# A decoder block on one core: x1 filled by its own transfer, out rows on ScalarE, a_ylo on VectorE, and a new order of steps

## What is computed

```python
x = x + attn(layernorm(x), w_attn, w_proj)              # 16 heads, causal linear attention, phi = elu + 1
x = x + xattn(layernorm(x), ctx, ctx, W_diff, ...)      # tanh-probabilities of q and ctx, softmax(-sid / 16) @ ctx,
                                                        # W_diff, layernorm, MLP 256-1024-256 with gelu, layernorm
x = x + ffn(layernorm(x), w_router, W_qkv, ...)         # out = h, but the 128 of 256 rows with the highest router
                                                        # score are replaced by h + attention + gated MLP of them
```

## Time and profile before

| | |
|---|---|
| median of 3 runs | 922.85 us (919.57, 922.85, 923.87) |
| profiled execution | 919.85 us; its span, first to last instruction, 918.0 us |
| PE busy | 817.0 us, 89% of the span |
| DVE busy | 725.8 us, 79% |
| ACT busy | 577.3 us, 63% |
| POOL busy | 301.5 us, 33% |
| DMA | 39.82 MB, 43 GB/s over the span (292 GB/s in the first fortieth) |
| granted TensorE clock | 0.98 of full speed on the mean |

### The profile page before, as it was taken

How to read it: one execution, slowest core, us unless ns; L and a number is a source line. 1 busy time by engine, 2 the same in 40 slices (tenths; PEclk the granted TensorE clock), 3 DMA queues, 4 the chain that set the end, 5 groups by cost and what they waited for, 6 DMA issues and landing times.

```text
span 918.0 us, 21136 instructions
## 1 busy us (share of the span) xinstructions
PE 817.0 (89%) x7222; PEld 705.6 (77%) x7222; DVE 725.8 (79%) x1609; ACT 577.3 (63%) x1550; POOL 301.5 (33%) x443
## 2 busy tenths in 40 slices
...
GB/s 292 84 47 1 59 24 47 41 35 48 6 81 6 57 29 46 40 29 51 6 80 6 57 29 46 40 29 51 6 80 6 57 29 46 30 2 46 6 53 7
DMA packets 26871, 39.82 MB, mean 43 GB/s; under 512 B 2256, under 2 KB 18768, under 8 KB 26832
## 3 DMA queue, kind: packets, MB, share of 16 engines
...
## 4 chain that ended last, share of the span: by engine, by line
PE 35%; DVE 22%; issue 17%; POOL 11%; ACT 10%; DMA 3%; POOLq 1%; SPq 0%; DVEq 0%; ACTq 0%
PE bank L1117 10%; DVE a_s L867 4%; PE bank L1239 3%; ACT w_raw_or_stage_c L712 3%; PE bank L1221 2%; DMA x_in<-in_x 2%; PE bank L1301 2%; ACT L712 2%; PE bank L1309 2%; PE bank L1401 2%; PE bank L1279 2%; PE bank L1385 2%; PE bank L1396 2%; POOL f_rs L436 1%; DVE prob L908 1%
## 5 line engine op out<-in xcount | busy, mean ns | idle before, releaser
L675 ACT ACTIVATE prob<-bank,b_folded 128x256 f32<-128x256 f32 x128 | 53.8, 471 | 111.4 <-PE bank L1117 111.2
L867 DVE TENSOR_TENSOR a_s<-bank,const 128x512 f32<-128x512 f32 x112 | 72.6, 685 | 40.0 <-PE bank L1239 21.7
L712 ACT ACTIVATE w_raw_or_stage_c<-bank,c_nmax 128x128 f32<-128x128 f32 x256 | 91.7, 406 | 3.2 <-DVE c_nmax L1037 3.0
L451 POOL TENSOR_TENSOR a_tr_lo<-a_norm,a_tr_hi 128x512 fp32r<-128x512 f32 x16 | 20.6, 1285 | 141.2 <-ACT a_tr_hi L562 141.2
L712 ACT ACTIVATION_READ_ACCUMULATOR w_raw_or_stage_c<-bank,c_nmax 128x1 f32 x256 | 62.7, 245 | 0.0
L784 DVE TENSOR_TENSOR b_s_lo<-prob,b_s_hi 128x512 fp32r<-128x512 f32 x64 | 44.9, 701 | 17.3 <-ACT b_s_hi L562 17.3
L427 POOL TENSOR_TENSOR q_bias<-b_f,vectors_by_row 128x512 f32<-128x512 f32 x16 | 20.6, 1285 | 114.4 <-DVE b_f L933 114.4
L1037 DVE TENSOR_REDUCE c_nmax<-bank 128x4 f32<-128x512 f32 x64 | 41.1, 685 | 21.0 <-PE bank L1401 21.0
L857 DVE RECIPROCAL a_e<-a_e 128x512 f32<-128x512 f32 x16 | 53.5, 3346 | 0.0
...
L1117 PE MATMUL bank<-b_s_hi,w_mlp_hi 128*128 128x256 f32 x256 | 45.1, 298 | 2.7 <-ACT prob L675 1.4
L1117 PEld LDWEIGHTS bank<-b_s_hi,w_mlp_hi 128*128 128x128 f32 x256 | 34.4, 188 | 13.0 <-issue 10.4
...
## 6 DMA issues: line engine op xcount, KB each, us to landing
...
```

Source lines behind the costliest of these rows:

```text
L675: act_in(prob[:, 2 * (j % 2) + n, :], b0[:, n * T:(n + 1) * T], ACT.Gelu, bias=b1p[:, f:f + 1]).then_inc(b_gelu.sem, 1)
L712: act_in(c_e[g % 2][:, j * R:(j + 1) * R], C_SCORES[g][:, j * R:(j + 1) * R], ACT.Exp, bias=c_nmax[:, n:n + 1], accum_out=c_den[:, head:he ...
L867: tt(heads(A_MASKED[t][n][:, :]), heads(A_SCORES[n][:, :]), tri.unsqueeze(1).broadcast_to([P, 4, P]), ALU.mult).then_inc(a_scput.sem, 1)
```

## The change

Four things are changed at once:

1. `x1` is no longer copied by GpSimd. SP loads it from memory a second time (`keep_x`), once at the start, and then behind `b_kept` and `b_normed` of the sequence before. `next_x` no longer waits for the copy.
2. `c_ob` moves to ScalarE. x2 + (x2 - mean) * r is computed as x2 * (1 + r) - mean * r in two activations with a factor and an offset per row; GpSimd makes factor and offset in a new step `c_obs` of three small instructions.
3. `a_ylo` moves to VectorE.
4. `ORDER` is new, and with it the places in `WARM_AT` (72 matmuls before, 74 after). `WEIGHTS_AT` is the same table.

```diff
+            sp.dma_start(x1[:, :, :], x_rows[0]).then_inc(a_kept.sem, 16)      # behind the loads of raw, ahead of ctx
...
             def next_x(b):
                 sp.wait_ge(*a_normed(b))
                 sp.sem_inc(passed.sem, 1)
-                sp.wait_ge(*a_kept(b))
+                sp.dma_start(xin[:, :, :], x_rows[b + 1]).then_inc(x_in.sem, 16)
+
+            def keep_x(b):
+                sp.wait_ge(*b_kept(b - 1))
                 sp.sem_inc(passed.sem, 1)
-                sp.dma_start(xin[:, :, :], x_rows[b + 1]).then_inc(x_in.sem, 16)
+                sp.wait_ge(*b_normed(b - 1))
+                sp.sem_inc(passed.sem, 1)
+                sp.dma_start(x1[:, :, :], x_rows[b]).then_inc(a_kept.sem, 16)
...
                 store(i - 2)
+                keep_x(i)
                 next_ctx_t(i - 1)
...
-            def a_kept_(b):                                                     # gpsimd
...
-                nc.gpsimd.tensor_copy(x1[:, :, :], xin[:, :, :]).then_inc(a_kept.sem, 1)
...
-            def a_ylo_(b):                                                      # gpsimd
-                pool.wait_ge(*a_yhi(b))
-                low(flat(a_tr[1][:, :, :]), flat(a_norm[:, :, :]), flat(a_tr[0][:, :, :]), a_ylo)
...
-            def c_ob_(b):                                                       # gpsimd
-                pool.wait_ge(*c_normed(b))
...
-                nc.gpsimd.tensor_tensor(ob[:, :, :], x2, c_norm, ALU.add).then_inc(c_ob.sem, 1)
+            def c_obs_(b):
+                pool.wait_ge(*c_rstd(b))
+                if not first(b):
+                    pool.wait_ge(*c_ob(b - 1))
+                pool.sem_inc(passed.sem, 1)
+                nc.gpsimd.tensor_scalar(c_gain[:, :], c_rs[:, :], 1.0, None, ALU.add).then_inc(c_obs.sem, 1)
+                nc.gpsimd.tensor_tensor(c_offset[:, :], c_mv[:, :, 0], c_rs[:, :], ALU.mult).then_inc(c_obs.sem, 1)
+                pool.wait_ge(*c_obs(b, 2))
+                pool.sem_inc(passed.sem, 1)
+                nc.gpsimd.tensor_scalar(c_offset[:, :], c_offset[:, :], -1.0, None, ALU.mult).then_inc(c_obs.sem, 1)
...
+            def c_ob_(b):                                                       # scalar
+                act_e.wait_ge(*c_obs(b))
+                if not first(b):
+                    act_e.wait_ge(*out_done(b - 1))
+                for t in range(TT):
+                    act_in(ob[:, t, :], x2[:, t, :], ACT.Identity, bias=c_offset[:, t:t + 1], scale=c_gain[:, t:t + 1]) \
+                        .then_inc(c_ob.sem, 1)
...
+            def a_ylo_(b):                                                      # vector
+                dve.wait_ge(*a_yhi(b))
+                low(flat(a_tr[1][:, :, :]), flat(a_norm[:, :, :]), flat(a_tr[0][:, :, :]), a_ylo)
...
                     dve.wait_ge(*c_rms1(b - 1))                                 # c_mean
+                    dve.wait_ge(*c_obs(b - 1))
...
-                    dve.wait_ge(*c_ob(b - 1))                                   # c_normed
```

One line of `ORDER` each, the part of a round with `c_idx` and `b_dtp`:

```diff
-a_val c_idx a_qout b_diff b_frstd+ b_dtp c_put++ c_gu_1+ b_rtp a_rstd a_ylo+ c_rank b_log c_gu_2+ c_gtp_0+
+c_idx c_gu_1+ b_vput b_dtp c_normed b_diff c_h2sq+ c_rscore b_rtp c_h2hi+ b_vq c_rank c_gu_2+ c_hx+ c_sel
```

More of the change, by code:

```diff
@@ L44 @@
 ORDER = """
-c_w2 a_kput+ c_ff_0++ c_ff_1++ c_gtlo_1++ c_rstd+ c_ht+ a_score_0+ b_fput+ b_fmean+ b_htp+ a_sput+ c_hsc+
-b_sexp+ c_gthi_0++ b_fnormed+ c_gthi_1++ a_mask+ a_mean a_dput+ c_w7 a_scput_0+ b_hlo+ a_scput_1+ c_qk+
-c_hput+ c_w1 b_up_0+ a_scput_2+ a_scput_3+ a_score_1+ c_w3 c_y++ c_rms1+ c_v+ a_scput_4+ b_hhi+ a_att_0+ c_w4
-c_qkput+ b_gelu_0+ a_scput_5+ a_scput_6+ b_up_1+ a_scput_7+ a_att_1+ b_ghi_0+ b_gelu_1+ b_glo_0+ a_dinv+
-c_vput+ a_y+ b_glo_1+ b_ghi_1+ b_down_0+ b_up_2+ b_gelu_2+ c_score+ b_up_3+ c_w8 a_proj+ a_yhi+ b_ghi_2+ c_w9
@@ L50 @@
-c_h2rms++ c_max_0+ c_max_1+ b_down_1+ b_down_2+ b_gelu_3+ b_qb+ c_etp_0+ c_max_2+ c_exp_0+ c_hx++ b_down_3+
-b_glo_2+ a_done+ c_max_3+ b_ghi_3+ c_exp_1+ c_etp_1+ c_ob+ b_v b_mean c_exp_2+ a_tp b_glo_3+ a_normed b_normed
-b_kept+ c_etp_2+ c_etput_0+ c_w0 c_exp_3+ c_w5 b_o+ c_etp_3+ c_dtp+ c_att+ b_omean+ b_onormed+ c_dinv+ b_done+
-c_etput_1+ c_xo+ c_dbc+ c_mean c_keep+ c_pick+ c_o+ c_etput_2+ a_tlo c_etput_3+ c_normed c_h2put+ c_dput+ a_q
-a_thi b_tanhk b_tanhq c_h2tp+ a_kept+ c_h2sq+ a_k c_rscore b_pnorm c_sbc c_gu_0+ c_h2lo+ b_vput b_fb2+ c_h2hi+
@@ L55 @@
-a_val c_idx a_qout b_diff b_frstd+ b_dtp c_put++ c_gu_1+ b_rtp a_rstd a_ylo+ c_rank b_log c_gu_2+ c_gtp_0+
-c_sel a_ktp b_vq b_sid c_gtp_1+ a_state b_rstd b_fd c_idxput b_orstd+ c_tanh_0+ a_kout b_ratio c_gate_0+
-a_phi_q a_phi_k b_dput c_gate_1+ b_rput c_w6 a_csum a_kq c_gtlo_0+ c_tanh_1+ a_den a_vput
+c_qk+ c_gtlo_1++ b_up_0+ c_w2 a_kput+ a_score_1+ c_hsc+ a_sput+ b_fnormed+ a_scput_0+ a_mask+ a_scput_1+
+b_hlo+ a_dput+ c_v+ c_hput+ b_frstd+ a_scput_2+ a_scput_3+ c_w7 b_hhi+ a_mean a_att_0+ c_w1 a_scput_4+ c_y++
```

37 lines of the change are left out of this document (22 added, 15 removed).

## The result

| | before | after |
|---|---|---|
| median, first comparison | 922.73 us (919.57 to 923.87, 4 runs) | 890.44 us (888.23 to 896.51, 4 runs) |
| ratio | | 0.9665 (95%: 0.962 to 0.9709) |
| the changed kernel again (e1) | 920.00 us | 889.39 us, ratio 0.9660 (0.9628 to 0.9692) |
| a round in the loop | 51.65 | 49.62 |

The forecast was 908.2 us with a range of 895 to 922: the direction is right, the size is wrong. 13 us were forecast, 31 to 32 came.

The account below looks back on a forecast made before the run. TensorE was taken to bound a round (48.13 of 51.68 us busy). Thirteen rounds at -1.2 (-15.6), fill -0.9 and drain +3.2 gave -13.3, from 921.5 to 908.2 us; range 895 to 922.

Parts of the forecast that it names:

- The two waits of 0.55 (b_dtp) and 0.79 (a_ktp): TensorE's waits for the copied-out index and for kT; both were to go in each round, -0.55 and -0.79.
- b_diff: VectorE step, to take 0.7 beside a short GpSimd instruction instead of 1.45 beside a long one.
- c_max_1 and c_dinv: VectorE steps: c_max_1 done at 451.7, about when ScalarE comes to the exponentials; c_dinv delays b_done 0.8; both priced 0.
- The wait for b_s_lo: New TensorE wait of 0.4 at the last pass of b_down_3, from VectorE's longer queue behind c_max_0.
- The lock rival: b_diff waits up to 0.7 for a short GpSimd instruction; scores late at c_sbc, +0.6 a round: 916.6 us; chance 0.04.
- c_att: TensorE's attention product: its 0.52 wait takes up the 0.4 delay of b_v; together 0, at worst +0.4; summed as -0.05.
- c_idx: TensorE's wait for VectorE's selections: 0.65 instead of 0.42 in a round, +0.2.
- The free selections: Rival: VectorE has the ranks out before TensorE reaches c_idx; 14 rounds x -0.65 = -9, so 899 us; chance 0.19.
- fill: Start before the loop: x1 load +0.9, a_ylo 0.6 shorter, step from sequence 1 to 2 gains 1.2; together -0.9.
- The x1 transfer's +0.9: In the fill, the extra 256 KB of x1 go ahead of the MLP's weights, for which ScalarE waits: +0.9.
- drain: After the loop: c_h2rms ahead of c_rms1 makes the last round 3.6 later, index wait gone -0.4; together +3.2.

Follow-up runs that it names:

- e13: The changed kernel with c_hx ahead of c_obs on GpSimd, so that it runs beside the two selections: 890.33 us, ratio 0.9669.
- e7: The changed kernel with a_tp's four transposes back behind b_v, ahead of c_etp_2, as before the change: 894.64 us, ratio 0.9751.
- e5: The kernel before, old order, with the three moves; on GpSimd c_obs behind c_hx and the pick ahead of b_kept: 922.73 us, ratio 1.0042.
- e6: The kernel before with only TensorE's queue changed: c_gu_1 ahead of b_dtp, b_sid and gate transposes ahead of a_ktp, b_fd ahead of a_state: 923.93 us, ratio 1.0072.

## Why the prediction was wrong

**Right.** Faster, by waits in the loop, with TensorE as the bound. The two waits of 0.55 (b_dtp) and 0.79 (a_ktp) went as forecast, b_v and c_xo kept their waits, b_diff sank to 0.68, c_max_1 and c_dinv cost nothing. The wait for b_s_lo is 0.16 in the round shown, the last pass starts 0.31 later than before against the 0.4 forecast. The lock rival is out: c_sbc does not wait in the loop. By luck the stretch up to c_att came out right, too: -0.05 was forecast and -0.06 measured (18.66 and 18.60), but as the sum of two things that the forecast did not have.

**Wrong: c_idx.** The step was "the ranks at 467.95 instead of 467.4, and `c_idx` at about 468.8. TensorE is there at 468.15, so it waits 0.65: +0.2". From the round's start the ranks were forecast at 27.89 and came at 27.86; TensorE was forecast at 28.09 and started c_idx at 28.26. What failed is what lies between: the walk gave the selections and their hand-over 0.85, since "the selections have only `c_hx` beside them", and it took 0.40. The prediction says itself that c_obs stands "ahead of `c_hx`", and it is c_obs's short instructions that run beside the selections, which took 0.42. e13 puts c_hx there and gets 0.80 and a wait of 0.46. So the term was not +0.2 but -0.42: that is the wait in each of the thirteen rounds. The 0.65 that the earlier trace rows give on the mean (10.4 in 16) has the 2.72 of round 2 in it; for the loop alone the view has

```profile
PE bank L1359 <- DVE select_by_token L1014: 5.5, 13, 0.5
```

The free selections stood among the rivals, with a chance of 0.19, and not in the sum.

**Wrong: c_att.** "So the 0.4 is taken up by the wait of 0.52 at `c_att`" treats this wait as a cushion. It is none: the copy that c_att waits for waits itself for TensorE's transposes (457.58 in e7's section), so whatever makes b_v late makes these and c_att late as well. And I overlooked that a_tp's 0.60 of TensorE work had moved from behind b_v, where it stood ahead of these transposes, to just ahead of c_dtp, that is into the wait. e7 undoes only this: 0.42 a round. The new delay (b_v starts 0.38 later from the round's start) and this gain nearly cancel, which is the luck named above.

With -0.42 and -0.42 instead of +0.2 and -0.05, and 0.4 for the delay, the sum of a round is -1.8; measured -2.03. The waits do not add up this simply, though. Behind c_idx the round lost 1.74 where the two terms there are 1.34, although c_gu_2's new wait must be paid from the same stretch, and e13 puts 0.46 of wait back for 0.18 of round. What gives the other 0.4 or more behind c_idx is in no wait that the view lists, and stays open.

**Wrong: fill.** -1.2 was given to the step from sequence 1 to 2; it gained 6.4. Before, TensorE waited 2.72 at c_idx and then ran at 1.2 GHz for more than half of 12 us (clocks of 0.71 and 0.72), here PE in two stretches of before's round 2:

```profile
104.00:110.00 6.00, 2.75 (x14) 0.71 0.15 50
110.00:116.00 6.00, 5.53 (x20) 0.72 0.15 44
```

The forecast took the waits of the steady round and did not look at this stretch. The x1 transfer's +0.9 may well be real: ScalarE waits 6.5 ahead of the first split of the MLP's weights (the row) on the mean of the eleven profiles with the transfer, and 5.6 on the mean of the five without, but the five alone spread from 4.6 to 6.2.

**Mis-sized: drain.** The order of c_h2rms and c_rms1 costs 2.0 instead of 3.6, since c_h2sq was ready 1.3 after c_rstd's start and not 3.2 after. Of the 6.7 by which e1's drain is longer, the other 4.8 are what lies between it and e7's, whose clock stayed up.

**What the sum hid.** The terms were treated as independent. They are not: order alone +1.0 a round, moves alone +0.5 (e5, as I placed the steps there), both -2.0. The two terms I was surest of gave nothing in the old surroundings (e6, +0.2). They held in the changed kernel, where b_sexp stands ahead of a_kput and nothing holds the selections and b_ratio; no run undoes one of the two in the changed kernel.
